# A spare readout product in every unit of a state-space scan on TensorE

## The reference

```python
def step(h, inp):
    dA_t, dB_t, x_t, C_t, t = inp
    h = h * dA_t + dB_t * x_t[:, :, None]
    nrm = jnp.sqrt(jnp.sum(h * h, axis=(1, 2), keepdims=True))
    fac = jnp.minimum(20.0 / (nrm + 1e-08), 1.0)
    h = jnp.where(t % 10 == 0, h * fac, h)
    y = jnp.einsum('bdn,bn->bd', h, C_t) + D_param * x_t
```

## Time and profile before

| what | value |
|---|---|
| median of 3 runs | 1732.75 us (1728.92 to 1733.2) |
| the profiled execution's own time | 1729.7 us |
| its span, first to last instruction | 1727.9 us |
| mean granted clock of TensorE | 0.897 |
| PE busy in the span | 1403.9 us (81%), 6362 matmuls |
| DVE busy | 1420.5 us (82%) |
| ACT busy | 1317.5 us (76%) |
| POOL busy | 975.1 us (56%) |
| the scan in the trace | 443 to 1480 us, granted clock 0.85 |

### The profile page before, as it was taken

The page is one execution under the profiler, slowest core; times in us unless marked ns, Lnnn a source line. Parts: engine busy times, 40 slices in busy tenths (PEclk is TensorE's granted clock), DMA queues, the critical chain, the costliest instruction groups (busy, mean ns, idle before and its releaser), DMA issues.

```text
span 1727.9 us, 23094 instructions
## 1 busy us (share of the span) xinstructions
PE 1403.9 (81%) x6362; PEld 1080.8 (63%) x6362; DVE 1420.5 (82%) x1698; ACT 1317.5 (76%) x3384; POOL 975.1 (56%) x1318
## 2 busy tenths in 40 slices
PE   6999999996388778777777787777777777898987
PEld 5555555552276667666666677666666666676765
DVE  7666776565799999999999999999999999676773
ACT  5376666779899999999999999999999965223232
POOL 1301222220588888888888888888888887200000
PEclk9999999999678897989888888888988887899998
DMA  7223353333323333333333243343323337335430
GB/s 233 74 74 123 101 156 118 111 106 112 92 76 104 95 95 87 93 98 81 94 92 97 74 108 79 97 102 90 98 75 92 85 104 204 108 104 164 129 110 25
DMA packets 202688, 179.78 MB, mean 104 GB/s; under 512 B 82816, under 2 KB 175040, under 8 KB 202560
## 3 DMA queue, kind: packets, MB, share of 16 engines
q1 hardware_dynamic: 201616, 176.99, 36.3%
q10 hardware_dynamic: 944, 1.31, 0.2%
HBM read 125.26 MB, written 53.57 MB: 103 GB/s over the span
## 4 chain that ended last, share of the span: by engine, by line
PE 41%; ACT 29%; POOL 10%; DVE 9%; issue 9%; DMA 1%; ACTq 0%; POOLq 0%; SPq 0%; DVEq 0%
ACT tb L959 13%; PE banks L915 10%; ACT decay L987 7%; POOL hc L874 6%; PE banks L347 6%; PE banks L339 5%; ACT sc_sq L970 5%; PE banks L1238 4%; PE banks L1249 3%; PE banks L314 3%; DVE h L1076 3%; PE banks L1218 3%; DVE cv L612 3%; POOL rc L866 3%; PE banks L898 2%
## 5 line engine op out<-in xcount | busy, mean ns | idle before, releaser
L1076 DVE TENSOR_TENSOR_SCAN h<-decay,banks 128x704 f32<-128x704 f32 x410 | 661.1, 1612 | 27.1 <-ACT banks L995 23.7
L915 PE MATMUL banks<-hc,w_ident 128*128 128x160 f32 (+1 forms) x3296 | 662.5, 354 | 17.0 <-POOL hc L874 13.2
L915 PEld LDWEIGHTS banks<-hc,w_ident 128*128 128x128 f32 x3296 | 569.6, 227 | 39.5 <-POOL hc L874 29.2
L874 POOL TENSOR_TENSOR hc<-h,bc 128x640 f32<-128x640 f32 x410 | 589.7, 1439 | 0.0
L959 ACT ACTIVATE tb<-dtc,a 128x320 f32<-128x320 f32 (+1 forms) x832 | 449.5, 556 | 0.0
L898 PE MATMUL banks<-sc_ss,sc_ones 128*128 128x1 f32 x820 | 167.0, 273 | 244.9 <-ACT sc_sq L970 232.4
L1064 DVE TENSOR_TENSOR banks<-banks,bc 128x640 f32<-128x640 f32 x410 | 341.3, 833 | 30.1 <-DVE h L1076 0.9
L898 PEld LDWEIGHTS banks<-sc_ss,sc_ones 128*128 128x128 f32 x820 | 145.2, 220 | 330.0 <-ACT sc_sq L970 327.7
L987 ACT ACTIVATE decay<-tb 128x640 f32<-128x640 f32 x410 | 298.3, 728 | 0.4
L866 POOL TENSOR_TENSOR rc<-qs,w_mhalf 128x1 f32<-128x1 f32 x410 | 224.8, 548 | 61.5 <-POOL qs L861 1.3
L257 POOL TENSOR_TENSOR ln_rz<-ln_vz,w_mhalf 128x4 f32<-128x4 f32 x8 | 13.9, 1734 | 281.2 <-DVE ln_vz L585 281.2
(11 more groups left out here) (110 smaller groups left out, 1629.6 us busy)
## 6 DMA issues: line engine op xcount, KB each, us to landing
bc<-scratch_blk SPq DMA_DIRECT2D x205, 320.0 KB, 3.4
uc<-scratch_u SPq DMA_DIRECT2D x35, 240.0 KB, 4.3
scratch_xc<-xc SPq DMA_DIRECT2D x8, 1024.0 KB, 4.8
scratch_sg<-sg SPq DMA_DIRECT2D x8, 1024.0 KB, 5.9
scratch_dt<-dt SPq DMA_DIRECT2D x8, 1024.0 KB, 5.6
scratch_u<-u SPq DMA_DIRECT2D x8, 1024.0 KB, 6.6
q_ys<-scratch_y SPq DMA_DIRECT2D x8, 1024.0 KB, 6.6
q_xc<-scratch_xc SPq DMA_DIRECT2D x8, 1024.0 KB, 8.9
```

Of the source, the lines that this page charges most:

```text
L874: pool.tensor_tensor(hc[:, pl % 2, :, j % 2 * S:(j % 2 + 1) * S] .rearrange("p (c b n) e -> p c b n e", c=KE, b=B)[:, :, b], state(m)[:, : ...
L915: mm = pe.matmul(psY[:, 0:KE * B * wide], w.ident[:], rhs, start=(n == 0), stop=(n == N - 1))
L1076: dve.tensor_tensor_scan(state(m).rearrange("p r e -> p (r e)"), decay[:, m % DRING], psI[m % B][:, 0:NCH * W], 0.0, ALU.mult, ALU.add).th ...
```

## The change

In `tensor` of `scan_stage`, each unit's quarter of the readout is issued as three products, then a new function `repeat`, then the fourth product. `repeat` waits for `q_copied` of the total just issued, and multiplies the identity with state 0 of the same pair's `hc` (the first of quarter 0's products, whichever quarter it is in) into columns 128 to 287 of `psQ`, bank 4. Nobody reads these columns, and nothing is signalled. It is issued in the units 4 to 407, 404 times.

```diff
@@ -917,6 +917,13 @@
+        def repeat(p, m):
+
+
+            pe.wait_ge(q_copied, m + 1)
+            rhs = hc[:, p % 2].rearrange("p (c n) t -> p c n t", n=N)[:, :, 0]
+            pe.matmul(psQ[:, P:P + KE * B * 2 * S], w.ident[:], rhs, start=True, stop=True)
+
@@ -929,7 +936,10 @@
             if p >= 0:
-                readout(p, quarter * 4, quarter * 4 + 4)
+                readout(p, quarter * 4, quarter * 4 + 3)
+                if m + B < UNITS:
+                    repeat(p, m + B)
+                readout(p, quarter * 4 + 3, quarter * 4 + 4)
```

## The result

| | before | changed |
|---|---|---|
| median | 1730.84 us (1722.98 to 1733.2, 4 runs) | 1702.66 us (1695.74 to 1704.96, 4 runs) |
| ratio | | 0.9836, 95% interval 0.9804 to 0.9868 |
| the profiled execution's own time | 1729.7 us | 1695.74 us |
| its scan, first to last start of a scan | 443.4 to 1478.5 us | 443.7 to 1454.4 us |
| from there to its end | 249.4 us | 239.5 us |

The change made the kernel 28 us faster. The page of the changed kernel shows the clock first; it answers to rows 1.

The account below looks back on a forecast made before the run. DVE was taken to bound the scan at full clock, and PE, narrowly, at low clock. Gains of 15.5 + 1 + 0.5 = 17 us gave 1712.7 from the profiled execution or 1715.8 from the median, taken as 1714 us; range 1705 to 1727.

Parts of the forecast that it names:

- What bounds the kernel: In the scan: DVE at full clock, 2.42 us a unit; PE, narrowly, while the clock is low.
- The product is hidden at full clock: On PE in the scan: about 0.28 us per product fits in idle time before the next total, cost zero.
- The clock: TensorE's clock in the scan: nearly all falls go, granted clock between 504 and 1380 us above 0.97.
- rival A: Low stretches of the scan: falls stay and each costs more, +25 to +54 us, 1765 us as one number; chance 0.11.
- What it gives back: Scan from 504 to 1400 us: 25 us lost, less 9 for boundaries and about 0.5 for opening units, leaves 15.5 us.
- these are ACT's and stay: Chunk boundaries in the scan: 11 at 0.79 us each, 9 us, held to be unchanged and left out of the gain.
- the slack of the loop: Between the carry's end and its scan: some 0.2 us, beyond which a late total or norm delays DVE.
- The scan's gain: Whole scan: 15.5 us in the middle, 1 in the opening and 0.5 near the end, 17 us in all.
- The 15.5 us for the low clock: Scan between 504 and 1400 us: the time lost to the low clock, expected to come back.
- B: Quarter 0 of the scan: falls go, but 0.2 us beyond cover and slack, 102 times, returns 20 us; 1725 to 1735; chance 0.10.
- C: Boundaries and opening chunk of the scan: carry less often late, more gain, 1702 to 1707 us; chance 0.05.

Follow-up runs that it names:

- The wait alone: Changed kernel with the wait for q_copied kept in every unit and the repeated matmul left out: 1734.41 us, ratio to before 1.0021.
- The halves of a chunk: Changed kernel, product repeated only in the 16 units after a chunk's boundary: 1717.65 us; only in the 16 ahead of one: 1712.52 us.
- the two products: Changed kernel with two spare products of 160 columns in each unit instead of one: 1704.18 us, ratio to before 0.985.
- the second profile of the changed kernel: The changed kernel run again without any edit, for another profile: 1702.17 us, ratio to before 0.9849.
- half a product: Changed kernel with the spare product cut from 160 to 80 columns: 1744.46 us, ratio to before 1.0078.

## Why the prediction was right in kind and wrong in size

**What bounds the kernel: right.** DVE paces the scan at full clock, and 12 scans still lie 2.42 to 2.43 us apart. PE sets the pace only in the low stretches.

**The product is hidden at full clock: right.** It holds PE for 0.27 us against 0.28 taken, and leaves 0.12 us after quarter 0 against 0.06 to 0.11. The bank change and the wait cost nothing that shows.

**The clock: right, and it was the open bet.** From 504 to 1380 it is granted at 1.00 where above 0.97 was forecast. The wait alone shows that it is the product that does it. Whether it is the added work or the shorter idle time ahead of the next total that counts was not separated: every product did both. The rule of the Trainium skill cited for rival A ("TensorE: Matmul & The Clock Gate", section "HAM oscillation — how this bites in real kernels"), that falls come from long waits with nothing to do, does not describe this scan: a little more work inside each unit removed every fall between 504 and 1380. In the last stage 4 slow runs do stand behind waits, of 2.56 us, and there were none when these were filled.

**What it gives back: the step that failed.** The sum said that 11 boundaries cost 0.79 us each, "and these are ACT's and stay". They did not stay: with the clock up they cost 2.67 - 2.42 = 0.25 us each. 11 x (0.79 - 0.25) = 5.9 us were left out of the gain on this ground. Behind it stands a misreading one step earlier. The 0.2 us between the carry's end and its scan was taken for the slack of the loop. It is a level that falls and rises. At 800 us it was 0.35 us; then a late norm on POOL, at full clock, took it to 0.14, in rows 3 it is 0.23 and on its way up, and by 826 us it is 0.52. In the changed kernel it stands at 0.76 to 0.80 us ahead of each of the 11 boundaries. The boundary of rows 8 was read as a price of ACT's extra tanhs, when it was that price less a reserve that falls, and the boundary before, had used. The halves of a chunk and the two products show it directly.

The scan's gain was put at 17 us. The profiles have 1035.1 - 1010.8 = 24.3 us. 5.9 us of the 7.3 between them are the boundaries. Of the rest, 0.8 us is the one unit near the end that waits for a DMA, 5.5 us long now and 6.4 before. That is chance: it is 3.9 us long in the second profile of the changed kernel. The 15.5 us for the low clock itself came out about right.

**The last stage: a term that had no place in the sum.** In the profiled pair it is 9.9 us shorter. The second profile of the changed kernel has it 4.4 us shorter, and all profiles without spare work there scatter over 11 us. The medians differ by 28 us, which leaves 28 - 24.3 = 4 us for this stage and for the scatter. Whether any of it is the change's doing is open.

**The rivals.** A did not happen, but its price was real, as half a product shows. B did not come: even two products are paid for by the reserve. C named the right place, with 0.05 as its chance: the carry less often late at the boundaries, 1702 to 1707 us. It deserved more. The trace of the kernel before already held the answer. The boundary of rows 8 has a lead of 0.21 us and a distance of 3.21. The one after it follows right behind rows 4, at full clock as well:

```profile
825.87 0.38 ACT L995 ACTIVATE banks<-h,rc 128x64 f32<-128x64 f32 x1
826.77 1.61 DVE L1076 TENSOR_TENSOR_SCAN h<-decay,banks 128x704 f32<-128x704 f32 x1
829.27 0.36 ACT L995 ACTIVATE banks<-h,rc 128x64 f32<-128x64 f32 x1
829.66 1.62 DVE L1076 TENSOR_TENSOR_SCAN h<-decay,banks 128x704 f32<-128x704 f32 x1 [0.42 <-ACT banks L995]
```

Here the lead is 0.52 us and the distance 2.89. One such comparison would have shown that the distance isn't fixed.

## What to carry to other kernels

Where TensorE's granted clock falls now and then and the engine has idle time in every round of the loop, spare matmuls into columns that nobody reads can hold it up; they must be hidden at full clock, and enough of them, for half a dose made the low stretches dearer and took away only a quarter of them. A wait that comes once per chunk is not a fixed price: set the lead of the late engine ahead of it beside its length at several places, and if their sum is nearly constant, whatever removes disturbances elsewhere will shorten it as well. When two profiles are compared, look at each stage, since one that the change doesn't touch moved here by 10 us.

## What was not expected of the hardware

The clock fell and rose in a loop in which TensorE idles no more than 1.09 us ahead of an undisturbed unit's total, and 0.27 us more work per 2.42 us unit ended this, while half as much raised the granted clock only from 0.87 to 0.90. The falls of an unchanged stage vary from execution to execution, with 239.5 and 245.0 us for the last stage of the same kernel.
